# A new order for the first slot of an eight-layer transformer kernel: activation table and first norm ahead, constant matmuls in TensorE's waits, bias products in another bank

## What is computed

```python
x = x + attn(layernorm(x))      # 8 layers
x = x + moe(layernorm(x))       # 8 experts, the best 2 of each token

def layer(h):                    # attn: h through 8 of these, then one more norm
    q = elu(h @ wq + bq) + 1     # 16 heads of 8
    k = elu(h @ wk + bk) + 1
    v = h @ wv + bv
    kv = einsum('bshd,bshm->bhdm', k, v)
    z = 1.0 / (einsum('bshd,bhd->bsh', q, k.sum(axis=1)) + 1e-6)
    h = ln(h + einsum('bshd,bhdm,bsh->bshm', q, kv, z) @ wo + bo, g1, be1)
    return ln(h + gelu(h @ w1 + c1) @ w2 + c2, g2, be2)
```

## Time and profile before

| | |
|---|---|
| median of 3 runs | 1067.89 us (1067.46 to 1069.88) |
| profiled execution, its own time | 1067.03 us |
| its span | 1065.3 us, 25018 instructions |
| TensorE busy | 997.0 us (94%) |
| VectorE busy | 830.9 us (78%) |
| ScalarE busy | 831.4 us (78%) |
| GpSimd busy | 770.0 us (72%) |
| mean granted TensorE clock | 0.976 of 2.4 GHz |

### The profile page before, as it was taken

The page is one execution under the profiler, slowest core; times in us unless marked ns, Lnnn a source line. Parts: engine busy times, 40 slices in busy tenths (PEclk is TensorE's granted clock), DMA queues, the critical chain, the costliest instruction groups (busy, mean ns, idle before and its releaser), DMA issues.

```text
span 1065.3 us, 25018 instructions
## 1 busy us (share of the span) xinstructions
PE 997.0 (94%) x7558; PEld 932.4 (88%) x7558; DVE 830.9 (78%) x2733; ACT 831.4 (78%) x1621; POOL 770.0 (72%) x1157
## 2 busy tenths in 40 slices
PE   5899999999999999999999999999998859989993
PEld 4799989999999999989999999899997759889993
DVE  6777887888888878887888788787889888953545
ACT  5878887888888888888888888888887645765582
POOL 5866877787877778777777777777766677677753
PEclk9999999999999999999999999999999878999997
DMA  4101263136314432443144315501302345667363
GB/s 140 51 1 36 55 130 60 36 75 111 59 38 96 90 59 42 99 90 60 40 100 100 63 42 122 95 8 21 100 1 80 93 130 162 178 190 219 102 182 129
DMA packets 196371, 92.81 MB, mean 87 GB/s; under 512 B 119788, under 2 KB 179187, under 8 KB 196112
## 3 DMA queue, kind: packets, MB, share of 16 engines
q1 hardware_dynamic: 190352, 81.71, 32.9%
q0 software_dynamic: 4544, 8.47, 2.3%
q10 hardware_dynamic: 1344, 1.05, 0.3%
HBM read 42.98 MB, written 31.54 MB: 70 GB/s over the span
## 4 chain that ended last, share of the span: by engine, by line
PE 72%; POOL 6%; DVE 6%; issue 5%; DMA 4%; SPq 4%; ACT 2%; DVEq 0%; POOLq 0%; ACTq 0%
PE psum L1943 19%; PE psum L1820 8%; PE psum L1822 8%; PE psum L1821 8%; PE psum L1867 6%; PE psum L1901 5%; PE psum L1873 5%; PE psum L1855 4%; PE psum L2102 4%; POOL xs L929 4%; PE psum L2086 4%; SPq L508 3%; DMA this_w<-w 2%; DVE stat L1240 1%; PE psum L1964 1%
## 5 line engine op out<-in xcount | busy, mean ns | idle before, releaser
L1026 ACT ACTIVATE s<-s,shift,rstd 128x128 f32<-128x128 f32 x496 | 203.9, 485 | 40.7 <-POOL shift L761 40.3
L1943 PE MATMUL psum<-this_w,hid 128*128 128x128 f32 x1792 | 216.5, 277 | 3.0 <-DMA this_w<-w 3.0
L1943 PEld LDWEIGHTS psum<-this_w,hid 128*128 128x128 f32 x1792 | 208.5, 193 | 4.2 <-DMA this_w<-w 4.2
L1005 ACT ACTIVATE hid<-psum,col 128x512 f32<-128x512 f32 x256 | 155.2, 683 | 2.3 <-PE psum L1822 1.7
L759 POOL TENSOR_TENSOR rstd<-var,neg_half 128x4 f32<-128x4 f32 x132 | 146.3, 1108 | 11.0
L802 POOL TENSOR_TENSOR res_a<-s,row 128x512 f32<-128x512 f32 x60 | 77.4, 1290 | 73.6 <-ACT s L1026 68.4
L1240 DVE BATCH_NORM_STATS2 stat<-s 128x6 f32<-128x128 f32 x512 | 110.0, 277 | 0.0
L756 POOL TENSOR_SCALAR shift<-mv 128x4 f32<-128x4 f32 x132 | 25.8, 195 | 100.1 <-DVE mv L1244 98.8
L1820 PE MATMUL psum<-x_hi,this_w 128*128 128x512 f32 x224 | 95.5, 426 | 1.2 <-DVE x_lo L1312 1.2
L787 POOL TENSOR_TENSOR res_f<-res_f,row 128x512 f32<-128x512 f32 x64 | 92.3, 1443 | 5.0
L2102 PE MATMUL psum<-heads,hid 128*128 x624 | 86.7, 284 | 6.8 <-ACT hid L1158 5.6
(11 more groups left out here) (270 smaller groups left out, 2761.3 us busy)
## 6 DMA issues: line engine op xcount, KB each, us to landing
xs<-pad SPq DMA_DIRECT2D x18, 975.0 KB, 8.8
feature<-xrow SPq DMA_DIRECT2D x416, 32.0 KB, 2.0
res_a<-w SPq DMA_DIRECT2D x28, 256.0 KB
xblk<-xs SPq DMA_DIRECT2D x78, 65.0 KB
row<-rows SPq DMA_DIRECT2D x8, 512.0 KB, 5.4
raw_w<-w SPq DMA_DIRECT2D x15, 256.0 KB, 3.0
this_w<-next_w SPq DMA_DIRECT2D x7, 512.0 KB, 3.2
this_qkv<-next_qkv SPq DMA_DIRECT2D x6, 384.0 KB, 2.9
```

The source lines that it names most:

```text
L1005: a.activation(hid[h][:, c, :], ps(3 + h + c), ACT.Gelu, bias=col[:, bass.ds(lw * FF + (C_C1 + c), 1)]).then_inc(hid_done, 1)
L1026: ins = a.activation(dst[:, t, :], src[:, t, :], ACT.Identity, bias=shift[i][:, t:t + 1], scale=rstd[i][:, t:t + 1])
L1943: ins = t_.matmul(ps(down_bank(l, s, h))[:, t * P:(t + 1) * P], hid[h][:, c, t * P:(t + 1) * P], down[:, c, :], start=c == 0, stop=c == FF ...
```

## The change

It touches the front of the program and slot 0 of layer 0 alone.

- **ScalarE**: an `Exp` of one column on a constant comes first, with it the table load; it signals `exp_table`, so that the later counts go up by one. Then `start(0)`, and only then the copy of the high part of the first `this_qkv`; `start_split(0)` comes ahead of `start(1)`.
- **VectorE**: `start_lo(0)` goes ahead of `start(2)`. `start(4)`, `start(5)` and `start(6)`, which stood ahead of slot 0, go into it: behind `keys(0)`, behind `keys(1)` and behind `mask_kv(1)`. `start(7)` goes from behind `keys(1)` to behind `attend(1)`.
- **TensorE**: `keep_clock(n)` issues `n` products of the constant `ones` with itself into bank 3, which nobody reads; 16 of them stand first, 4 behind `bias_products(0)`. `project(0, 0, 0)` is issued ahead of `start(1)`, and `project(0, 0, 1)` directly behind it.
- **Banks**: the bias products of layer 0 go to bank 6, and `project(0, 0, 0)` no longer waits for `bias_done`. `start(2)`, which transposes into bank 6, waits for it instead.

GpSimd's and SyncE's streams have the same order as before, and so has ScalarE's from the norms of halves 2 and 3 on: the copies of halves 4 and 5 still stand behind the norm of half 7.

```diff
+        def bias_bank(l):
+            return 1 if l else 6
...
# block.scalar
+            act.wait_ge(const_step, 7)
+            a.activation(warm[:, 0:1], ones[:, 0:1], ACT.Exp).then_inc(exp_table, 1)
+            start(0)
             act.wait_ge(raw_in, 32)
             a.activation(this_qkv[:, 0, :], raw_qkv[:, :], ACT.Copy).then_inc(qkv_split, 4)
-            start(0)
+            start_split(0)
             start(1)
-            start_split(0)
             start_split(1)
...
-                load_table(ACT.Exp, 1, exp_table, l * SLOTS + s)
+                load_table(ACT.Exp, 1, exp_table, l * SLOTS + s + 1)
...
# block.vector
-                b = ps(1)
+                b = ps(bias_bank(l))
...
+            start_lo(0)
             start(2)
             start(3)
-            start_lo(0)
             start_lo(1)
             biases(0, 0)
-            start(4)
-            start(5)
-            start(6)
...
                 keys(l, s, 0)
+                if first and s == 0:
+                    start(4)
                 keys_values(l, s, 1)
...
                 keys(l, s, 1)
                 if first and s == 0:
-                    start(7)
+                    start(5)
...
                 mask_kv(l, s, 1)
+                if first and s == 0:
+                    start(6)
                 attend(l, s, 0)
                 attend(l, s, 1)
...
                 if first and s == 0:
+                    start(7)
                     start_lo(4)
                     start_lo(5)
...
# block.tensor, project
-                elif h == 0 and ((s == 3 and not last) or (first and s == 0)):
-                    wait(pe, bias_done, l * 8 + (16 if s == 3 else 8))
+                elif h == 0 and s == 3 and not last:
+                    wait(pe, bias_done, l * 8 + 16)
...
# block.tensor, start(u)
-                if 4 <= u < 6:
+                if u == 2:
+                    pe.wait_ge(bias_done, 8)
+                elif 4 <= u < 6:
...
+            def keep_clock(n):
+                for _ in range(n):
+                    t_.matmul(ps(3)[:, 0:P], ones[:, :], ones[:, :], start=True, stop=True)
+
+            pe.wait_ge(const_step, 7)
+            keep_clock(16)
+            pe.wait_ge(const_done, 1)
             start(0)
+            bias_products(0)
+            keep_clock(4)
+            project(0, 0, 0, True, False)
             start(1)
-            bias_products(0)
+            project(0, 0, 1, True, False)
...
-                project(l, s, 0, first, last)
-                project(l, s, 1, first, last)
+                if not first or s > 0:
+                    project(l, s, 0, first, last)
+                    project(l, s, 1, first, last)
```

More of the change, by code:

```diff
@@ L1972, in router_bias @@
                 t_.matmul(ps(1)[:, EXPERTS:2 * EXPERTS], ones[:, :], r_sc[:, :], start=True, stop=True).then_inc(rb_mm, 1)
-            pe.wait_ge(const_done, 1)
             def start(u):
                 pe.wait_ge(x2_done, u + 1)
-                if 4 <= u < 6:
+                if u == 2:
+                    pe.wait_ge(bias_done, 8)
+                elif 4 <= u < 6:
                     pe.wait_ge(xt_lo_done, u - 1)
```

## The result

| | before | changed |
|---|---|---|
| median of 10 runs each, taken side by side | 1066.58 us (1064.68 to 1069.88) | 1070.61 us (1068.94 to 1074.48) |
| ratio, 95% interval | | 1.0046 [1.003, 1.0062], +4.9 us (3.2 to 6.6) |
| both kernels again, later | 1064.23 us (19 runs) | 1072.29 us (6 runs), 1.0073 [1.0047, 1.0099] |
| profiled execution, own time | 1067.03 us | 1070.61 us |

The account below looks back on a forecast made before the run. TensorE, 94% busy with no slack behind slot 1, was taken as the bound, so slot 1's start decides. Half 7's wait (+4.8) and the restart clock (+2.3), rounded to +7.0 us, gave a median of 1074.9 us, range 1070.3 to 1079.5.

Parts of the forecast that it names:

- No slack behind slot 1: TensorE after slot 0: a shift of its work in slot 0 or 1 reaches the end nearly one for one.
- Step 1: Front, ScalarE: first norm begins at 6.7 instead of 7.53 us, ending 0.8 us sooner; constant products cause no delay.
- Step 2: Front, TensorE: projections earlier, project(0, 0, 1) done 4.7 us sooner, but VectorE's keys(0) only at 20.2 instead of 22.61 us.
- Step 3: VectorE in slot 0: three halves' statistics make the stretch 11.7 us, ending at 32.3; of 2.4 us won, 0.5 left.
- Step 4: Ahead of the first output projection: TensorE waits for half 7's whole chain, starting at 39.0 instead of 34.20, +4.8 us.
- Step 5: TensorE's restart after some 6 us idle: half clock from 39.0 to 42.9 us, +2.3 us.
- What costs nothing: GpSimd's later weights and residuals, 6.1 us behind, are covered by the output projections with 2 us; bias bank is free.
- The sum: Whole kernel: +4.8 and +2.3 make +7.1, rounded down to +7.0 us; profiled execution 1074.0 us, median 1074.9 us.
- Rival D: Smaller loss: no clock fall at the restart, weight load's wait takes some; +2.7, 1070.6 us; chance 0.12.
- B: Rival: clock falls already at the front, during bias products and first projection; in all +11.4, 1079.3 us; chance 0.10.
- C: Rival: clock stays down until slot 1's projections, transposes at half clock too; +9.5, 1077.4 us; chance 0.10.

Follow-up runs that it names:

- e6: Kernel before the change, with SyncE's load of w2 ahead of its load of the next layer's rows: 1062.59 us, ratio 0.9967.
- e7: Changed kernel, with SyncE's load of w2 ahead of its load of the next layer's rows: 1067.59 us, ratio 1.0009.
- second trace: Profile of the changed kernel run once more, nothing edited: 1072.29 us, ratio 1.0073; profiled execution 1068.79 us.
- e1: Changed kernel, with ScalarE's copies of halves 4 and 5 and both attention copies ahead of half 7's norm: 1069.51 us, ratio 1.003.
- e3: Changed kernel, with VectorE's statistics of halves 4 to 7 back where they stood before: 1063.31 us, ratio 0.9977.
- e4: Kernel before the change, with only VectorE's statistics of halves 4 to 7 at the change's places: 1072.94 us, ratio 1.0064.
- e5: Changed kernel without the 16 and the 4 constant products at the front: 1078.45 us, ratio 1.0104.
- e11: e10 with six more constant products in TensorE's wait ahead of the first output projection: 1059.23 us, ratio 0.9953.
- e10: Changed kernel with VectorE's statistics back, w2 load first, and six constant products each side of slot 0's key_value: 1059.63 us, ratio 0.9955.

## Why the prediction was right

- **No slack behind slot 1: right.** The lag is constant from slot 1 of layer 0 to slot 1 of layer 1, and in e6 against e7 up to layer 7.
- **Step 1, the first norm: right.** 6.89 instead of 7.53, where I had 6.7; the 16 constant products ended at 6.91 (1.51 + 5.40), against 7.5, and at 7.98 in the second trace, still ahead of the transposes. The table load again ended 0.01 us ahead of the next ACTIVATE (0.81 + 1.28 against 2.10). The extra drain of the Trainium skill, "ScalarE: Activation LUTs", section "What ACT_TABLE_LOAD costs", does not show in this gap either. Nor does it at the 61 loads of the later slots: ScalarE's idle time ahead of all of them is 1.1 us together on the page of the changed kernel, and the ACTIVATE behind each begins 0.01 to 0.02 us after the load's end.
- **Step 2, projections: right.** `project(0, 0, 0)` at 11.50 (11.2 said), spacing 0.24; `phi_q` 17.92 (17.6), `keys(0)` 20.46 (20.2).
- **Step 3, VectorE gives it back: right, a little large.** `attend` ended at 32.07 (31.38 + 0.69), 32.3 said; from `keys(0)` 11.6 us, 11.7 said. The 0.4 us that I added for attention at half clock did not come in this trace, as VectorE never waited for attention, and the later start of `keys(0)` made up for most of it: that 32.3 is so near is in part luck. In the second trace VectorE waited 0.36 us there and ended at 32.68. The idle time ahead of the second `key_value` was 2.56, about 3 said.
- **Step 4, half 7's chain: right, and shown by runs from both sides.** Output projection at 38.70, 39.0 said: +4.5 instead of +4.8. The chain took 6.63 us; my terms add up to 6.5, and the 39.0 comes of rounding up on the way. e1 shows that it is ScalarE's order that carries it, e3 and e4 that the statistics' place sets it off.
- **Step 5, the clock at the restart: right in kind, +1.7 instead of +2.3, and the term was summed wrongly.** I had the half clock for 3.9 us (39.0 to 42.9); it was about 3.6 (38.70 to 42.28), and the transposes at 42.28 already ran at the full rate. But 3.9 us at half clock do 1.95 of the 2.68 us of work, and the remaining 0.73 goes at full clock: that is 4.6 us and +2.0, not 5.0 and +2.3. It took 4.4 us in the first trace; in the second and in e7 the transposes ran at half rate too, and it took 5.1.
- **"What costs nothing": right for this kernel, with less cover than I named.** The residual of half 1 was ready at about 40.6 (38.07 + half of 4.96), 40.8 said, and the output projections covered it. But the sentence that followed, "each further us on GpSimd would be one for gelu", missed the nearer one: had the output projection been on time, `add_res1` would have waited 5.04 us (e1). The same four blocks of statistics set off two waits of about the same size; one hid the other. Had I put e1's order in the place of the change, I would have forecast nearly no loss, and e1 lost 0.3%.
- **The sum: right at its place, uncertain in the time.** +7.1 was said for slot 1; the traces have +6.2, +7.6 (e7) and +7.6. In the time it is +4.9 and +7.8 in the two comparisons. The profiled execution took 1070.61 us, not 1074.0: 0.8 of the 3.4 us is slot 1, 1.1 came back up to layer 7, most of it by the waits for `w2`, of which I had said that they move along, and 1.5 behind the layers. The median of the first comparison, 1070.61, is inside the range by 0.3 us only, that of the second, 1072.29, by 2.0; the kernel before also stood 1.3 us lower in the first than in the three runs that I built on (1066.58 against 1067.89).
- **Rival D was right in one part.** The weight load took some of the lag in the first trace (3.2 us of it), and my argument against it ("SyncE issues that load behind the transposed blocks of an earlier half, so it moves along") holds for the issue only. The wait differs in every trace (the first of them, at about 160 us: 2.14 before, 0.63 and 0.21 in the two of the changed kernel), and the clock fell only behind the longest. The other part, no fall of the clock at the restart, was wrong. That D's 1070.6 us is the first median to the tenth is chance.
- **B did not occur, and C only in its smaller part:** at the front the full rate held, and behind the restart the first projection's matmuls are 0.4 long. The transposes, 0.4 of C's price, ran at half rate in the second trace and in e7. Whether transposes alone bring the clock up stays open: in the first trace it was up when they began, in the second they ran at half rate and the matmuls behind them at full, directly after the half-rate output projections.

Open: how TensorE's clock behaves at the front in the executions without a trace. The traces of one order of instructions differ by 1.4 us at slot 1, the ten times of the changed kernel in the first comparison by 5.5 us; how the two belong together was not tried. Nor is it known why e6 and e7 differ by 7.7 us in their traces and by 5.0 in their medians.

## What to carry to other kernels

Before work is moved out of the way of an engine, ask which engine that works in written order has something urgent behind the consumer of that work: here four ACTIVATEs of half 7 held copies that had nothing to do with it, and GpSimd's residuals stood in the same position. If two such rows hang on one moved producer, the trace shows the longer wait only, and the other appears when the first is mended. A lead at the start of a pipeline is worth only what the next engine in the chain can pass on: 4.8 us at the first projection became 0.4 to 1.0 us at slot 1, even with the loss mended.

## What was not expected of the hardware

- Constant products of float32 ones in a wait brought and kept the full rate: 0.24 instead of 0.42 us between 512-column matmuls at 12 us (e5 against the changed kernel), 1.98 instead of 3.68 us for the output projection (e11 against e10).
- At the front the granted clock of the records did not show the rate. In e5, with matmuls 0.42 apart, the row reads

```profile
12.00:14.00 2.00, 2.00 (x7) 1.71 (x8) 1.43 (x12) 0.00 (x0) 1.40 (x3) 1.00 0.19 59
```

  that is, 1.00. In that part of the program the spacing of the matmuls is what to read.
- A gap of nearly the same length had different ends: 1.64 us ahead of the output projection in e10, and 3.68 us for its 16 passes; 1.71 us in e1 and 2.05 us. In e10 TensorE had run fast for longer before the gap than in e1. That does not tell them apart either: in e6 it had run fast since 23 us, and behind a gap of 1.62 us the same 16 passes took 2.05. These runs don't show what makes the difference.
- One weight load that came 2.1 us late cost more than its wait: 2.14 us of waiting and 1.6 us more for 32 passes at the lower clock. Its place in SyncE's row is worth 0.33% (e6), the mended front 0.23% (e3); the intervals overlap.
